# A Mamba-2 mixer with a LoRA-routed linear layer on one core: two chunks of 256 tokens instead of four of 128, and another order of the products in a step

## The chip, the cores and the metric

The kernel runs on one core of a Trainium2 chip. Its time is the device time of one execution in microseconds. Engines are named as in the profile: PE is TensorE (matmul), PEld its weight loads, DVE is VectorE, ACT is ScalarE, POOL is GpSimd, SP is SyncE, which here only issues DMAs.

## What is computed

The input x is 2 x 512 tokens of 512 values. With xn its layer norm, the output is `x + mamba2(xn) + lora_linear(xn)`.

```python
proj = hidden_states @ in_proj_w.T                  # 512 -> 8192 gate + 10240 hBC + 128 dt
hBC = silu(causal_conv4(hBC) + conv_b)              # hs 8192, B 8 x 128, C 8 x 128
dt = softplus(dt + dt_bias)
A_cs = cumsum(A * dt, within a chunk)
Y_diag = (C B^T * exp(segsum(A dt))) @ (hs * dt)    # inside a chunk
states = (B * exp(A_cs[last] - A_cs))^T @ (hs * dt) # one 128 x 64 state per head and chunk
Y_off = (C @ state_before_the_chunk) * exp(A_cs)
y = Y_diag + Y_off + D * hs
xg = y * silu(gate)
out = (xg * rsqrt(mean over a group of 1024 (xg^2) + eps) * norm_weight) @ out_proj_w.T
```

There are 128 heads of 64 channels and 8 groups of B and C. The second summand is `xn @ W.T + b` plus a LoRA product whose rank (8, 16, 32 or 64) a softmax over four scores picks for each token. The length of a chunk is a free choice: the recurrence gives the same result for any.

## The kernel before

A batch (there are 2, index b) is one sequence of 512 tokens. All its tokens lie side by side in the free dimension, so most operations are 512 columns wide. A large product is made in three parts from high and low halves in fp32r (`three`, L505: hi x hi, hi x lo, lo x hi, each in KT = 4 blocks, twelve PE instructions). `project` (L519) makes 128 channels of the input projection for 512 tokens. Scans, states, score and Y products and transposes are in fp32. Every matmul in fp32 is two PE instructions in the profile, a transpose is one.

A **prologue** per batch makes dt, its soft log and the cumulative sums (`csT`, by a scan over `chunked`, which restarts every 128 tokens), the LoRA part, and for 8 groups g the conv of B and C and the **scores** (L558, score products `bo[2]<-h2,ct`, masked on DVE by `causal` into `gt`). Tables by token follow: `cs_tok`, `dt_tok`, `dd_tok` (decay to the chunk's end times dt) and `cd_bc` (decay over a chunk).

The **step loop** has 64 steps per batch, two heads (128 channels) each. It is software pipelined: PE's pass m, called slot m here, holds the projections of step m, the scan of step m-1 and the output product of step m-2. Each engine runs its own list of instructions in the order in which they are written, with semaphores between them; that order is all that sets what stands behind what. In a slot PE does (before the change):

1. **hs** product, `project(bh, ...)`, L509 by its helper's line, then **states**: `bt<-xd,btok` (L635), one 128x128 product for each of the first three chunks (NS = 3), then **Y**, `by<-mt,xt` (L641): for four blocks j of 128 tokens and two heads h a product with 64 stationary columns, into the upper or lower half of the bank;
2. **gate** product, `project(bg, ...)`, then **off**: `bt<-ct,S` (L657), three products of 128 columns with the running states S;
3. after every eighth step the sums of squares, `bt<-ones,sqa` (L662), into the last columns of `bt`;
4. **output** product of step m-2, `bo<-woh,xh` and the two mixed ones (L676), twelve instructions, accumulated over eight steps in four banks bo;
5. four **transposes** of the conv's result, `bt<-ident,h` (L687; the tile `h2` is printed as `h`).

[...]

DVE does in slot m: `xd` and `xt` (L868, L873), conv taps (L701), running states `next_state` (L726), y1 = D * hs + Y (L894), `silu_conv` (L707), the gate's `sg` (L908), `yo`, its addition and `xg` (L915, L918, L922), the **mask** mt * gt (L928, both heads in one instruction), and after each group `add_group` (L719), which empties the four output banks into `acc`. ACT does the last tap (L282), eight Relu pieces of the decay exponents (`rises`, L291), exp over them (L390), tanh of conv and gate (L287, L401), the copy of the first state S (L385), the high halves `xh`, `woh`, `wh` (L364, L407, L278), the norm weight on the output weights (L396) and the squares (L370). POOL makes the low halves `xl`, `wol`, `wl` (L479, L491, L440), the sum of squares (L486) and the inverse root (L446). SP issues the loads of weights and of the rows `cs_row` and `ec_row`, broadcast from DRAM.

## Time and profile before

| | us |
|---|---|
| median of 3 runs (lowest, highest) | 1695.9 (1695.87, 1696.78) |
| the profiled execution | 1696.02 |
| its span in the trace | 1694.3 |
| PE busy | 1644.4 (97%) |
| DVE, ACT, POOL busy | 1352.8, 1191.2, 1089.1 |

Matmuls overlap: a row of n of them lasts from the start of the first to the end of the last, and the time from one row's start to the next row's start is what they cost PE. A timeline merges neighbouring instructions of the same line, operation and tile into one row with their count. "idle before" in brackets is the time for which the engine had nothing to do ahead of the row, and what ended it.

### The profile page before, as it was taken

Reading aid. Unit: us, or ns where it says so; the run is one execution under the profiler, and the core shown is the slowest. Engines: PE = TensorE matmul, PEld = TensorE weight load, DVE = VectorE, ACT = ScalarE, POOL = GpSimd, SP = SyncE. Lnnn points to the kernel's source line nnn. Section 1 sums busy time; section 2 is a strip of 40 time slices with the busy share of each in tenths; the row PEclk is TensorE's granted clock in tenths of the full one; section 3 lists DMA queues with packets and bytes.
Section 4 is the critical chain, followed back from the end, with each engine's and each line's share of the span. In section 5 each row is a group of like instructions: output and inputs, shape, how many; then the busy total and the mean of one; then the engine's idle time right before and its main releaser. Section 6 shows DMA issues by size and latency. Waiting matters only on the chain.

```text
span 1694.3 us, 28881 instructions
## 1 busy us (share of the span) xinstructions
PE 1644.4 (97%) x9694; PEld 1355.9 (80%) x9694; DVE 1352.8 (80%) x2388; ACT 1191.2 (70%) x2442; POOL 1089.1 (64%) x1384
## 2 busy tenths in 40 slices
PE   6999999999999999999899999999999999999996
PEld 5778888888888888887787788888888888888885
DVE  5987788878787888878889878888788878787875
ACT  2577777777777777777635777777777777777773
POOL 5346676676676677676663466776766676676673
PEclk9999999999999999999999999999999999999998
DMA  4243444343444344343123433443443443443331
GB/s 150 65 143 123 140 136 129 130 144 122 129 144 127 125 144 131 120 144 131 58 86 100 156 128 124 144 131 120 144 132 122 142 133 120 142 133 126 136 119 36
DMA packets 82146, 212.03 MB, mean 125 GB/s; under 512 B 11024, under 2 KB 27408, under 8 KB 81744
## 3 DMA queue, kind: packets, MB, share of 16 engines
q1 hardware_dynamic: 82000, 210.20, 38.1%
q8 instruction: 78, 1.28, 0.3%
q14 instruction: 68, 0.56, 0.1%
HBM read 207.01 MB, written 3.15 MB: 124 GB/s over the span
## 4 chain that ended last, share of the span: by engine, by line
PE 69%; DVE 19%; ACT 6%; issue 5%; POOL 0%; DMA 0%; SPq 0%; DVEq 0%; ACTq 0%; POOLq 0%
PE bg L509 18%; PE bh L509 16%; PE bo L676 15%; DVE cv L701 6%; PE by L641 6%; PE bt L635 4%; PE bt L657 4%; DVE mt L928 2%; PE bt L687 2%; DVE acc L719 2%; ACT raw_o L396 1%; ACT mt L390 1%; DVE xt L873 1%; ACT cv L282 1%; DVE by L918 1%
## 5 line engine op out<-in xcount | busy, mean ns | idle before, releaser
L440 POOL TENSOR_TENSOR wl<-raw,wh 128x256 fp32r<-128x256 f32 x584 | 530.6, 939 | 101.5 <-ACT wh L278 101.5
L491 POOL TENSOR_TENSOR wol<-raw_o,woh 128x256 fp32r<-128x256 f32 x256 | 184.3, 741 | 468.6 <-ACT woh L407 468.6
L701 DVE SCALAR_TENSOR_TENSOR cv<-bh,par_sb,cv 128x511 f32<-128x511 f32 (+2 forms) x408 | 304.6, 747 | 140.2 <-ACT cv L282 135.1
L291 ACT ACTIVATE mt<-cs_row,cs_tok 128x128 f32<-128x128 f32 x1024 | 324.4, 389 | 0.0
L676 PE MATMUL bo<-woh,xh 128*128 128x512 f32 x512 | 213.7, 417 | 0.0
L676 PE MATMUL bo<-woh,xl 128*128 128x512 f32 x512 | 202.6, 396 | 0.0
L676 PE MATMUL bo<-wol,xh 128*128 128x512 f32 x512 | 200.9, 392 | 0.0
L908 DVE SCALAR_TENSOR_TENSOR sg<-tg,bg 128x512 f32<-128x512 f32 x128 | 88.1, 688 | 140.6 <-ACT tg L401 140.6
L287 ACT ACTIVATE bh<-cv 128x512 f32<-128x512 f32 x136 | 81.9, 602 | 159.2 <-DVE cv L701 159.2
L479 POOL TENSOR_TENSOR xl<-xg,xh 128x256 fp32r<-128x256 f32 x256 | 181.7, 730 | 4.9 <-ACT xh L364 4.9
L364 ACT ACTIVATE xh<-xg 128x512 fp32r<-128x512 f32 x128 | 81.0, 633 | 142.8 <-DVE xg L922 142.8
L928 DVE TENSOR_TENSOR mt<-mt,gt 128x1024 f32<-128x1024 f32 x128 | 174.1, 1360 | 0.0
L509 PE MATMUL bh<-xTh,wh 128*128 128x512 f32 x552 | 163.8, 419 | 1.5 <-DVE xTl L759 1.5
L509 PE MATMUL bg<-xTh,wh 128*128 128x512 f32 x544 | 161.8, 419 | 0.0
L486 POOL TENSOR_TENSOR sqa<-sqa,sq 128x256 f32<-128x256 f32 x224 | 160.6, 738 | 0.0
L278 ACT ACTIVATE wh<-raw 128x1024 fp32r<-128x1024 f32 (+1 forms) x146 | 152.8, 1046 | 0.7 <-DMA raw<-in_w_dtag 0.7
L282 ACT ACTIVATE cv<-bh,par_sb 128x512 f32<-128x512 f32 x136 | 105.7, 777 | 66.3 <-PE bh L509 61.3
L509 PE MATMUL bh<-xTl,wh 128*128 128x512 f32 x552 | 150.6, 395 | 0.0
L509 PE MATMUL bh<-xTh,wl 128*128 128x512 f32 x552 | 148.7, 391 | 0.0
L509 PE MATMUL bg<-xTl,wh 128*128 128x512 f32 x544 | 146.8, 391 | 0.0
L509 PE MATMUL bg<-xTh,wl 128*128 128x512 f32 x544 | 146.2, 390 | 0.0
L641 PE MATMUL by<-mt,xt 128*64 128x128 f32 x2048 | 141.0, 280 | 0.0
(159 smaller groups left out, 3328.3 us busy)
## 6 DMA issues: line engine op xcount, KB each, us to landing
raw<-in_w_step SPq DMA_DIRECT2D x128, 512.0 KB, 3.7
cs_row<-cs_rows SPq DMA_DIRECT2D x128, 512.0 KB, 4.5
raw_o<-in_w_out SPq DMA_DIRECT2D x128, 256.0 KB, 2.7
ec_row<-ec_rows SPq DMA_DIRECT2D x256, 96.0 KB, 3.7
raw<-in_w_bc SPq DMA_DIRECT2D x16, 512.0 KB, 3.6
acc<-in_x SPq DMA_DIRECT2D x2, 1024.0 KB, 5.7
mt<-in_w_ffn SPq DMA_DIRECT2D x2, 1024.0 KB, 6.7
out_dram<-acc SPq DMA_DIRECT2D x2, 1024.0 KB, 4.6
```

Source lines behind the costliest of these rows:

```text
L278: act.activation(wh[:, n % 2, 0:width(n)], raw[:, n % 2, 0:width(n)], ACT.Copy).then_inc(a_wh, 1)
L282: act.activation(cv[:, u, :], src[:, :], ACT.Identity, bias=par_sb[:, un % UNITS, TAPS:TAPS + 1], scale=par_sb[:, un % UNITS, TAPS - 1:TAP ...
L291: e = act.activation(mt[:, m % 2, h, chunk(j)], cs_row[:, m % 2, h, chunk(j)], ACT.Relu, bias=cs_tok[:, b, j, 2 * m + h:2 * m + h + 1], sc ...
L440: e = pool.tensor_tensor(wl[:, n % 2, part], raw[:, n % 2, part], wh[:, n % 2, part].bitcast(F32), ALU.subtract)
L479: e = pool.tensor_tensor(xl[:, u, part], xg[:, u, part], xh[:, u, part].bitcast(F32), ALU.subtract)
L486: e = pool.tensor_tensor(sqa[:, part], sqa[:, part], sq[:, part], ALU.add)
L491: e = pool.tensor_tensor(wol[:, 1 - u, part], raw_o[:, 1 - u, part], woh[:, 1 - u, part].bitcast(F32), ALU.subtract)
L509: mm = pe.matmul(dst, a(k), c(k), start=(n == 0 and k == 0), stop=(stop and n == 2 and k == KT - 1))
L641: mm = pe.matmul(by[HD * h:HD * (h + 1), chunk(j)], xt[:, j, HD * h:HD * (h + 1)], mt[:, 1 - u, h, chunk(j)], start=True, stop=True)
L676: mm = pe.matmul(bo[j][:, :], a[:, u, chunk(j)], c[:, u, :], start=(first and k == 0), stop=False, skip_group_check=True)
L701: dve.scalar_tensor_tensor(out=cv[:, u, k:], in0=src[:, 0:L - k], scalar=par_sb[:, un % UNITS, TAPS - 1 - k:TAPS - k], in1=cv[:, u, k:], o ...
L928: dve.tensor_tensor(mt[:, u], mt[:, u], gt[:, m % GROUPS, :].unsqueeze(1).broadcast_to([P, 2, L]), ALU.mult).then_inc(v_m, 1)
```

## The change

A chunk is now CL = 256 tokens long, so there are NC = 2 chunks. One state remains, that of the first chunk, so `next_state` and `cd_bc` go. `span(j)` is the block of query tokens that key block j reaches: 256 columns for the first block of a chunk, 128 for the second. `tri(j)` is its place in the packed lower triangle of TRI = 384 columns per chunk, in which `mt`, `gt` and `causal` now lie. Y accumulates two key blocks in the same columns. Off and what follows it (`yo`, its addition) cover the second chunk's 256 tokens alone, and off now goes to `bg`.

The hs product alternates between banks bh and bt (`mine`, `other`); states and transposes follow it there. On PE a slot's three fp32r products stand in a row, and all fp32 products behind them. DVE does yo, its addition and xg of step m-2 at the start of slot m and not at the end of slot m-1; the mask of step m-1 comes a slot later; the gate's sg ahead of the conv's h2; y1 last. ACT has the last tap ahead of the squares, both tanh after the first Relu pieces, and the copy of S behind tanh, norm scale and woh. POOL splits the next step's weights (`split_lo`) one step later and ahead of wol. In the prologue score products use the wider `span(j)`, transposes of B are two, the tables by token are made in three groups rather than two, and are no longer kept per batch. The four token transposes of the next batch and its `ag` product take the place of a projection in the last two slots; its norm statistics come a slot later.

```diff
@@ sizes and places
-NS = NJ - 1
+CL = 2 * P
+NC = L // CL
+TRI = CL + P
+        def span(j):
+            return slice(P * j, CL * (j // 2) + CL)
+        def tri(j):
+            return slice(TRI * (j // 2) + CL * (j % 2), TRI * (j // 2) + (CL if j % 2 == 0 else TRI))
@@ scores, PE
-                    mm = pe.matmul(bo[2][:, chunk(j)], h2[:, u, chunk(j)], ct[:, g, chunk(j)], start=True, stop=True)
+                    mm = pe.matmul(bo[2 + j // 2][:, CL * (j % 2):CL * (j % 2) + (P if j % 2 else CL)],
+                                   h2[:, u, chunk(j)], ct[:, g, span(j)], start=True, stop=True)
...
@@ step loop, PE
                     if has(m):
                         pe.wait_ge(p_wl, did(step(b, m)))
-                        project(bh, b, step(b, m) % 2, 0).then_inc(t_hs, 1)
+                        project(mine, b, step(b, m) % 2, 0).then_inc(t_hs, 1)
+                        if has(m - 2):
+                            pe.wait_ge(v_off, did(n - 2))
                         project(bg, b, step(b, m) % 2, 1).then_inc(t_g, 1)
+                    elif b + 1 < NB:
+                        pe.wait_ge(v_off, did(n - 2))
+                        if m == STEPS:
+                            for j in range(NJ):
+                                turn_tokens(b + 1, j)
+                        else:
+                            project_ag(b + 1)
...
                     if has(m - 2):
...
                         mm.then_inc(t_out, 1)
+                    if ends and m < STEPS:
+                        pe.wait_ge(v_sg, did(n))
+                        sum_squares(bg)
+                    if has(m - 1):
...
+                        for c in range(2):
+                            mm = pe.matmul(other[:, 0:P], btok[:, g, c, :], xd[:, c, :], start=(c == 0), stop=(c == 1))
+                        mm.then_inc(t_st, 1)
+                        pe.wait_ge(v_m, did(n - 1))
+                        pe.wait_ge(v_xg, did(n - 2))
+                        for j in range(NJ):
+                            for h in range(2):
+                                mm = pe.matmul(by[HD * h:HD * (h + 1), span(j)], xt[:, j, HD * h:HD * (h + 1)],
+                                               mt[:, 1 - u, h, tri(j)], start=(j % 2 == 0), stop=(j % 2 == 1),
+                                               skip_group_check=True)
+                        mm.then_inc(t_d, 1)
                     if m == STEPS and b + 1 < NB:
                         project_dt(b + 1)
+                    if has(m - 1):
+                        pe.wait_ge(v_sg, did(min(n, b * STEPS + STEPS - 1)))
+                        pe.wait_ge(v_off, did(n - 2))
...
+                        pe.wait_ge(a_s1, did(n - 1))
+                        pe.matmul(bg[:, CL:], S[:, :], ct[:, g, CL:], start=True, stop=True).then_inc(t_off, 1)
                     if has(m):
                         pe.wait_ge(v_h2, did(un))
                         for j in range(NJ):
-                            mm = pe.transpose(bt[:, chunk(j)], h2[:, u, chunk(j)], ident[:, :])
+                            mm = pe.transpose(mine[:, chunk(j)], h2[:, u, chunk(j)], ident[:, :])
                         mm.then_inc(t_t, 1)
@@ POOL
+                    if m >= -1 and (has(m + 1) or (m < STEPS + 1 and b + 1 < NB)):
+                        split_lo(step(b, m + 1))
                     if has(m - 1):
                         pool.wait_ge(a_woh, did(n - 1))
...
-                    if m + 2 < STEPS or (m < STEPS and b + 1 < NB):
-                        split_lo(step(b, m + 2))
```

On PE an ordinary slot of the step loop read so before (`woh`, `wol`, `xh`, `xl` are the output product's halves; eleven more rows like the last belong to it, and the four transposes come behind them):

```order
L509 MATMUL bh<-xTh,wh 128x512 [waits v_h2,p_wl]
L635 MATMUL bt<-xd,btok 128x128 [waits v_x,v_xd]
L635 MATMUL bt<-xd,btok 128x128 x2
L641 MATMUL by<-mt,xt 64x128 [waits v_xg,v_m]
L641 MATMUL by<-mt,xt 64x128 x7
L509 MATMUL bg<-xTh,wh 128x512 [waits v_sg]
L657 MATMUL bt<-ct,S 128x128 [waits v_s]
L657 MATMUL bt<-ct,S 128x128 x2
L676 MATMUL bo<-woh,xh 128x512 [waits p_wol,p_xl]
```

and reads so now:

```order
L516 MATMUL bh<-xTh,wh 128x512 [waits p_wl]
L516 MATMUL bg<-xTh,wh 128x512 [waits v_off,v_sg]
L670 MATMUL bo<-woh,xh 128x512 [waits p_wol,p_xl]
L683 MATMUL bt<-xd,btok 128x128 [waits v_x,v_xd]
L683 MATMUL bt<-xd,btok 128x128
L689 MATMUL by<-mt,xt 64x256 [waits v_xg,v_m]
L689 MATMUL by<-mt,xt 64x256
L689 MATMUL by<-mt,xt 64x128 x2
L689 MATMUL by<-mt,xt 64x256 x2
L689 MATMUL by<-mt,xt 64x128 x2
L701 MATMUL bg<-ct,S 128x256 [waits a_s1,v_off,v_sg]
L705 MATMUL bh<-ident,h 128x128 [waits v_h2]
```

Gate and output moved ahead of states, Y and off; states and off lost two matmuls each, half of Y's are wider, and off now waits for ACT's copy of S (a_s1) itself.

On ACT the same slot before, from the squares on:

```order
L370 ACTIVATE sq<-xg 128x512 [waits p_sqa]
L291 ACTIVATE mt<-cs_row,cs_tok 128x128 [waits t_d,ld_cs1]
L291 ACTIVATE mt<-cs_row,cs_tok 128x128 x3
L282 ACTIVATE cv<-bh,par_sb 128x512 [waits v_h2,t_hs]
L385 ACTIVATE S<-bt 128x128 [waits t_off,t_st]
L291 ACTIVATE mt<-cs_row,cs_tok 128x128 x4
L287 ACTIVATE bh<-cv 128x512 [waits v_tap]
L390 ACTIVATE mt<-mt 128x1024 [waits a_rl]
L396 ACTIVATE raw_o<-raw_o,par_sb 128x512 [waits ld_rawo0]
L401 ACTIVATE tg<-bg 128x512 [waits v_sg,t_g]
L407 ACTIVATE woh<-raw_o 128x512 [waits t_out,a_wn]
```

and now, where the rows of the second four Relu pieces (L299, like the first) and of exp over 1536 columns (L414) follow the last:

```order
L290 ACTIVATE cv<-bt,par_sb 128x512 [waits v_h2,t_hs]
L390 ACTIVATE sq<-xg 128x512 [waits p_sqa]
L299 ACTIVATE mt<-cs_row,cs_tok 128x256 [waits t_d,ld_cs1]
L299 ACTIVATE mt<-cs_row,cs_tok 128x128
L299 ACTIVATE mt<-cs_row,cs_tok 128x256
L299 ACTIVATE mt<-cs_row,cs_tok 128x128
L397 ACTIVATE tg<-bg 128x512 [waits v_sg,t_g]
L295 ACTIVATE bt<-cv 128x512 [waits v_tap]
L403 ACTIVATE raw_o<-raw_o,par_sb 128x512 [waits ld_rawo0]
L407 ACTIVATE woh<-raw_o 128x512 [waits t_out,a_wn]
L410 ACTIVATE S<-bh 128x128 [waits t_off,t_st]
```

The copy of S stood between the last tap and the second Relu pieces; it now stands behind the tanh that waits for DVE's taps, and behind norm scale and woh.

## Rows read from the trace of the kernel before

**Rows 1.** The page: busy time and share; granted clock in 40 slices; chain by engine.
```profile
PE 1644.4 (97%) x9694; PEld 1355.9 (80%) x9694; DVE 1352.8 (80%) x2388; ACT 1191.2 (70%) x2442; POOL 1089.1 (64%) x1384
PEclk9999999999999999999999999999999999999998
PE 69%; DVE 19%; ACT 6%; issue 5%; POOL 0%; DMA 0%; SPq 0%; DVEq 0%; ACTq 0%; POOLq 0%
```

**Rows 2.** Timeline, one ordinary slot, PE: start us, length us, engine, line, operation.
```profile
432.47 1.18 PE L509 MATMUL bh<-xTh,wh 128*128 128x512 f32 x4
...
435.34 0.91 PE L635 MATMUL bt<-xd,btok 128*128 128x128 f32 x6
...
436.17 1.09 PE L641 MATMUL by<-mt,xt 128*64 128x128 f32 x16
...
437.20 1.19 PE L509 MATMUL bg<-xTh,wh 128*128 128x512 f32 x4
...
440.05 0.83 PE L657 MATMUL bt<-ct,S 128*128 128x128 f32 x6
...
440.64 0.48 PE L676 MATMUL bo<-woh,xh 128*128 128x512 f32 x1
...
443.49 0.60 PE L687 MATMUL bt<-ident,h 128*128 128x128 f32 x4
...
443.85 0.48 PE L509 MATMUL bh<-xTh,wh 128*128 128x512 f32 x1
```

**Rows 3.** Timeline, three slots around the end of a group, PE and DVE.
```profile
385.89 1.18 PE L509 MATMUL bh<-xTh,wh 128*128 128x512 f32 x4
...
394.16 0.95 PE L662 MATMUL bt<-ones,sqa 128*128 128x1 f32 x8
...
398.17 1.17 PE L509 MATMUL bh<-xTh,wh 128*128 128x512 f32 x4
...
399.73 2.72 DVE L719 SCALAR_TENSOR_TENSOR acc<-bo,rr,acc 128x512 f32<-128x512 f32 x4
...
409.46 1.17 PE L509 MATMUL bh<-xTh,wh 128*128 128x512 f32 x4
```

**Rows 4.** Timeline, prologue of batch 0, PE: wide fp32, a projection behind another, scores.
```profile
54.45 3.70 PE L596 MATMUL bo<-w_b_sb,gt 64*128 64x512 f32 x8
...
60.97 1.07 PE L509 MATMUL bg<-xTh,wh 128*128 128x512 f32 x4
...
63.69 1.05 PE L558 MATMUL bo<-ct,h 128*128 128x128 f32 x8
```

**Rows 5.** Groups by line and shape, DVE: count, busy us, mean ns, idle before.
```profile
L928 DVE TENSOR_TENSOR mt<-mt,gt 128x1024 f32<-128x1024 f32 x128 | 174.1, 1360 | 0.0
L726 DVE SCALAR_TENSOR_TENSOR S<-S,cd_bc,bt 128x64 f32<-128x64 f32 x512 | 118.8, 274 | 4.3 <-ACT S L385 4.2
L701 DVE SCALAR_TENSOR_TENSOR cv<-bh,par_sb,cv 128x511 f32<-128x511 f32 x136 | 101.8, 749 | 135.1 <-ACT cv L282 135.1
...
L915 DVE TENSOR_TENSOR yo<-bt,ec_row 128x384 f32<-128x384 f32 x128 | 70.5, 551 | 0.4 <-PE bt L657 0.4
```

**Rows 6.** The same view, ACT.
```profile
L291 ACT ACTIVATE mt<-cs_row,cs_tok 128x128 f32<-128x128 f32 x1024 | 324.4, 389 | 0.0
...
L396 ACT ACTIVATE raw_o<-raw_o,par_sb 128x512 f32<-128x512 f32 x128 | 90.4, 706 | 0.0
L287 ACT ACTIVATE bh<-cv 128x512 f32<-128x512 f32 x136 | 81.9, 602 | 159.2 <-DVE cv L701 159.2
...
L407 ACT ACTIVATE woh<-raw_o 128x512 fp32r<-128x512 f32 x128 | 79.3, 619 | 0.1
...
L385 ACT ACTIVATE S<-bt 128x128 f32<-128x128 f32 x128 | 35.0, 273 | 15.4 <-PE bt L635 15.4
...
L356 ACT ACTIVATE cd_bc<-bo 128x256 f32<-128x256 f32 x2 | 0.8, 387 | 0.0
```

**Rows 7.** Timeline, PE, a slot near the end of batch 0.
```profile
806.24 1.62 PE L635 MATMUL bt<-xd,btok 128*128 128x128 f32 x6 [2.87 <-DVE xt L873]
```

**Rows 8.** Timeline, PE, the last sums of squares.
```profile
1679.79 1.65 PE L662 MATMUL bt<-ones,sqa 128*128 128x1 f32 x8 [2.75 <-POOL sqa L486]
```

More of the change, by code:

```diff
@@ L290, in rises @@
                 for j in range(NJ):
-                    e = act.activation(mt[:, m % 2, h, chunk(j)], cs_row[:, m % 2, h, chunk(j)], ACT.Relu,
-                                       bias=cs_tok[:, b, j, 2 * m + h:2 * m + h + 1], scale=-1.0)
+                    e = act.activation(mt[:, m % 2, h, tri(j)], cs_row[:, m % 2, h, span(j)], ACT.Relu,
+                                       bias=cs_tok[:, j, 2 * m + h:2 * m + h + 1], scale=-1.0)
                 e.then_inc(a_rl, 1)
@@ L330, in _ @@
                 act.activation(ecT, csT, ACT.Exp).then_inc(pa, 1)
[L331 to L334 removed]
+                act.activation(dec, csT[:, 0:CL], ACT.Exp, scale=-1.0, bias=csT[:, CL - 1:CL]).then_inc(pa, 1)
                 act.wait_ge(pe_, b * PRO_PE + PE_UT)
@@ L473, in _ @@
                     n, u = b * STEPS + m, m % 2
-                    if m == STEPS - 3 and b + 1 < NB:
+                    if m == STEPS - 2 and b + 1 < NB:
                         inverse_dev(b + 1)
@@ L616, in _, with sum_squares @@
                     n, un, u = b * STEPS + m, b * UNITS + 2 * GROUPS + m, m % 2
+                    mine, other = bank_s[u], bank_s[1 - u]
+                    ends = has(m - 2) and (m - 2) % PER_GROUP == PER_GROUP - 1
+                    def sum_squares(dst):
+                        pe.wait_ge(p_sqa, squares(b, m - 2))
+                        for j in range(NJ):
+                            mm = pe.matmul(dst[:, j:j + 1], sqa[:, chunk(j)], ones[:, 0:1],
+                                           start=True, stop=True)
+                        mm.then_inc(t_ss, 1)
@@ L793, in decays_and_route @@
                 dve.wait_ge(p_xl, did(b * STEPS - 1))
-                link(b, dve.tensor_tensor_scan(csT, chunked[:, :], dh, 0.0, ALU.mult, ALU.add))
+                for c in range(NC):
+                    part = slice(CL * c, CL * (c + 1))
+                    link(b, dve.tensor_tensor_scan(csT[:, part], ones[:, 0:1].broadcast_to([P, CL]), dh[:, part], 0.0,
+                                               ALU.mult, ALU.add))
                 assert done[b] == PRO_DVE_CS
```

335 lines of the change are left out of this document (143 added, 192 removed).

## The prediction

> **What bounds the kernel now.** I read the page's first and fourth parts first: TensorE has work 97% of the span at full clock, and its instructions carry 69% of the chain that ended last [rows 1]. Busy PE is not by itself proof, so I then followed one slot of the step loop on PE [rows 2]. Its seven phases follow one another without a gap: hs product 2.87 us, states 0.83, Y 1.03, gate product 2.85, off-diagonal 0.59, output product 2.85, transposes 0.36, together 11.38. Over the 128 slots the ordinary ones take 11.32 to 11.40 by the same two starts, mean 11.35; in every other one the states begin some 0.05 late, behind xt. DVE and ACT are busy 80% and 70% and wait inside the slot. So a PE instruction saved is time saved, for as long as nobody comes late to PE. Twice per group of eight steps a slot is longer: by 0.9 where the squares are summed, which costs PE 0.82, and then by about 0.35 where DVE empties the four output banks (slots of 12.28 and 11.29, then 11.72, counted from hs product to hs product) [rows 3].
>
> **What the change does to a slot on PE.** All fp32r products (hs, gate, output) now stand in one row, the fp32 ones (states, Y, off, transposes) in one row behind them.
>
> (1) States: three 128-column fp32 products become two. A product is two PE instructions here (768 records for 384 products). Eight such instructions in a row last 1.05 in all and one lasts 0.27, so they start 0.111 apart [rows 4]; six in 0.59 is 0.098 apiece [rows 2]. Two fewer: −0.21.
> (2) Off: three products of 128 columns become one of 256. Width 512 in fp32 is in the trace: eight instructions over 3.70, one lasting 0.59, so 0.44 apart, four times the narrow one's [rows 4]. A 256-column one then takes 0.21 to 0.22 and the pair 0.43, against 0.59: −0.16.
> (3) Y: sixteen 64x128 instructions in 1.03 [rows 2], 0.064 each, under the 0.107 that one of this width needs, so the two heads' halves of the array run side by side, eight pairs of 0.107. Four of the eight pairs get 256 columns: +4 × 0.107 = +0.43. The bounds: +0.34 if some of the 1.03 is fixed start-up hidden by wider ones, +0.64 if the two halves overlap only in part once their widths alternate. I take 0.43, since pairs are what the row shows.
> (4) Changes of kind. A projection that follows another starts its next three blocks 2.72 later (60.97 to 63.69) [rows 4], behind an fp32 phase the same blocks take 2.85; the output product takes 2.85 there too, of which its first instruction is 0.31 long instead of 0.23. Gate and output now follow fp32r work: −0.13 and −0.08. The hs product still follows the transposes and keeps its extra 0.1.
> (5) The 0.05 wait for xt goes: xt is now made some 6 us before the states want it. −0.04.
>
> Sum per slot: −0.21 −0.16 +0.43 −0.13 −0.08 −0.04 = −0.19; built up from the new order instead (2.84 + 2.72 + 2.77 + 0.56 + 1.46 + 0.43 + 0.36) it is 11.14, −0.21. I take −0.21: **128 × −0.21 = −27 us**. From the bounds of (3) and of (4) (nothing to −0.3): −0.33 to +0.05.
>
> Y still needs the array cut into two halves and put together again. Between the end of the pairs and the next phase there is about 0.1 that no product fills (16 instructions need 0.86 of the 1.03) [rows 2], and I leave it in. [...]
>
> **Who could come late.** Let 0 be the start of a slot's hs product; PE then starts gate at 2.8, output 5.6, states 8.3, Y 8.9, off 10.3, transposes 10.8, next slot 11.1.
> DVE. Off the list: 4 state updates of 0.23 net (four in 0.93) and a third of three 384-wide operations (0.55 to 0.42). Mask: 1.36 for 1024 columns becomes 1.9 to 2.0 for 1536 [rows 5]. Its new order is y1 behind Y (ready 10.4), yo, add, xg (to 1.4 of the next slot), xd, xt (2.35), mask (4.3), three taps of 0.75 (6.55), sg, h2 (7.9). It then idles 2.5.
> ACT. Eight Relu pieces of 0.39, half of them now 256 wide: 128 to 256 columns costs 0.11 at most by its row of 0.387 against 0.273 for a PSUM copy of 128, and up to double if I scale; exp of 1536 columns costs +0.43. So 9.4 becomes some 10.3 busy in 11.1 [rows 6]. Its queue is strict: gate tanh, **tanh of the conv (waits for the taps)**, norm scale, woh, **the copy of S**, and only then can PE do off. In an ordinary slot: taps ready 6.55, tanh to 7.15, scale and woh to 8.4, S waits for the states until 9.0, ready 9.3, against 10.3 wanted. A slack of 1.0, so nothing is paid.
> POOL: xl ready about 4, wanted 5.6; the split of the next step's weights (four of 0.94) moves ahead of wol and ends near 9.6, wanted 11.1. SP's weight load goes behind that split, near 9.6, and its 3.7 us to landing end 10 us before ACT wants it. Both hide.
>
> **(6) The slot in which the banks are emptied.** DVE does 4 × 0.68 = 2.7 more between xt and the mask [rows 3]. Taps end 9.25, tanh 9.9, scale 10.5 (0.71), woh 11.1 (0.62), S ready 11.4: off waits 1.05 to 1.1. Before, the same work cost 0.35 a slot later. 14 such slots (7 a batch): **14 × 0.72 = +10 us**. If the wait eats less, say 0.5, it is +2; the slot after it recovers (ACT is done with exp at 2.0, before the mask at 2.35).
> (7) Prologue of a batch: the score products cover 768 instead of 512 columns, +4 × 0.107 for each of 8 groups; one transpose less in each, −0.11; the products that spread the chunk decays go, −0.54 with one transpose. 2 × (8 × 0.32 − 0.54) = **+4 us**. PE is about as loaded there as DVE, whose mask grows by about as much.
> (8) End of batch 0. The slots where DVE also makes the next batch's norms are 14.3, 13.9 and 12.7, 6.9 over the ordinary; the first shows PE waiting 2.87 for xt [rows 7]. DVE has 1 us more room in each: I get some 3.3. Then all four token transposes stand ahead of the output product, two round trips PE-ACT-DVE-PE, with DVE's mask behind: +1.4. Net **−2 us**.
> (9) The very end. The last step's output product but one stood behind off and was hidden under the chain yo, xg, xh, xl, squares, for which PE waited 2.75 at the end [rows 8]. Now it stands ahead of the last states and off, in the chain: **+2.7 us**, its length.
>
> Sum: −27 +10 +4 −2 +2.7 = −12.3. The profiled execution took 1696.0 (span 1694.3), the median of the three runs 1695.9, so no correction is needed: **1684 us**.
>
> **Rivals.**
> A, *ACT's queue sets every slot* (slower). What (6) prices for 14 slots happens in all: from Y's end through y1, yo, add, xg, xd, xt, mask, taps, tanh, scale, woh, S to off is one chain of about 10.1 us round the loop, with 1.0 of slack. For it: ACT becomes 93% busy, and ten operations stand in that chain, each of which may be dearer than I take it. Against: no single wait in the walk is over. It decides once the chain is 1 us longer than I count; each 0.1 above costs 13 us. With 0.3 above: −12 + 38, 1722.
> B, *Y widens by 0.64 instead of 0.43* (slower): +0.21 × 128 = +27, 1711. For it: alternating widths and instructions that start in order. Against: both heads of a token block have the same width.
> C, *the changes of kind were not what cost the extra 0.2* (no change or slightly slower): gate and output keep their long first instruction, for instance since it is a first instruction after a semaphore wait. −12 + 27 = +15, 1711; if half stays, 1697, no change. Against: blocks that follow without such a change take 2.72 with a semaphore wait ahead of them as well.
> D, *more is won*: (6) is half hidden and Y costs 0.34: −12 −5 −11, 1668.
>
> **How the numbers follow.** Forecast with the size of (3), (4) and (6) as taken, 1677 to 1691: 0.50. D and between: 0.12. C's half, about 1697: 0.12. B, or C in full, 1700 to 1712: 0.14. A: 0.12. The predicted time is the first one's. Leaving out A and the far side of D gives 1667 to 1710. A measurement of this kernel tells some 0.2% (3.4 us) from no change: faster 0.62, same 0.12, slower 0.26.
>
> **What would show it.** Right: ordinary slots of 11.1 to 11.2 with phases 2.72 for gate, 2.75 for output, 0.43 for off, 1.45 for Y; the slots with emptied banks about 12.1, off waiting for ACT's S. Wrong: PE waiting for S in ordinary slots (A); Y at 1.65 (B); the first instruction of gate and output still 0.3 (C).

## The result, and the profile of the changed kernel

The change makes the kernel 0.2% slower. It takes 1699.95 us (median of 20 runs, 1697.19 to 1702.32), the kernel before beside it 1696.22 (20 runs, 1694.20 to 1699.27); the ratio is 1.0018, with a 95% interval of 1.0012 to 1.0025. The forecast was 1684, faster. The time lies in the range of the prediction, but the sign is wrong. The profiled execution of the changed kernel has a span of 1699.5. Of the experiments below, one execution of e2 (2336.4) and one of e3 (3308.5) were far slower than all others; they stand in no median.

The page, as [rows 1]: PE has lost 794 instructions and 10.5 us of busy time, and the span is longer all the same. The last slice of the granted clock has fallen from 8 to 7.
```profile
PE 1633.9 (96%) x8900; PEld 1316.1 (77%) x8900; DVE 1284.7 (76%) x1894; ACT 1327.9 (78%) x2436; POOL 1141.9 (67%) x1383
PEclk9999999999999999999989999999999999999997
PE 79%; DVE 12%; issue 4%; ACT 2%; POOL 2%; DMA 0%; SPq 0%; DVEq 0%; ACTq 0%; POOLq 0%
```

The timeline of one ordinary slot on PE, as [rows 2] (start, length, engine, line, operation):
```profile
444.89 1.17 PE L516 MATMUL bh<-xTh,wh 128*128 128x512 f32 x4
...
447.74 1.07 PE L516 MATMUL bg<-xTh,wh 128*128 128x512 f32 x4
...
450.46 0.39 PE L670 MATMUL bo<-woh,xh 128*128 128x512 f32 x1
...
453.21 0.60 PE L683 MATMUL bt<-xd,btok 128*128 128x128 f32 x4
453.74 1.52 PE L689 MATMUL by<-mt,xt 128*64 128x256 f32 x16
455.19 0.70 PE L701 MATMUL bg<-ct,S 128*128 128x256 f32 x2
455.73 0.60 PE L705 MATMUL bh<-ident,h 128*128 128x128 f32 x4
456.08 1.17 PE L516 MATMUL bt<-xTh,wh 128*128 128x512 f32 x4
```
From start to start: hs 2.85, gate 2.72, output 2.75, states 0.53, Y 1.45, off 0.54, transposes 0.35. That is 11.19 against a mean of 11.35 before: 0.16 gained in a slot, where 0.21 was forecast.

What PE waits for (microseconds in all, times, longest):
```profile
PE bg L701 <- ACT S L410: 17.1, 16, 1.1
...
PE bo L670 <- POOL xl L486: 7.7, 4, 5.0
PE bo L516 <- DVE acc L734: 2.5, 1, 2.5
```
Off waits for the copy of S in 16 slots: the 14 of the prediction's step (6), and in each batch the second slot, which it had not seen. The last row is the wait at the turn (e7). No ordinary slot waits for it.

**Where the time went.** I cut both kernels at the start of a step's transposes, T(0) to T(63) in each batch. Of both there is a second profile (e10 is before, e9 after), and the columns give both executions. T is the start of the instructions of L687 before and of L705 after.

| stretch | before, e10 | after, e9 | difference | predicted |
|---|---|---|---|---|
| start to T(0) of batch 0 | 110.78, 113.56 | 115.75, 113.56 | +2.2, see below | +2.0 |
| T(0) to T(1), each batch | 10.82, 10.85 | 9.61, 9.61 | 2 x -1.2 | 2 x -0.2 |
| T(1) to T(60), batch 0 | 678.41, 678.49 | 673.98, 674.11 | -4.4 | -7.4 |
| T(60) to T(63) | 40.96, 39.73 | 37.03, 37.06 | -3.3 | -3.9 |
| T(63) to T(0) of batch 1 | 103.69, 103.71 | 112.31, 112.36 | +8.6 | +3.2 |
| T(1) to T(63), batch 1 | 712.50, 712.44 | 707.78, 707.83 | -4.7 | -8.0 |
| T(63) to the end | 26.25, 26.18 | 33.44, 32.52 | +6.8 | +2.7 |

The differences sum to +2.8, the medians to +3.7; the last column sums to -11.8, the prediction's -12.3. The start must be compared at a like clock (the clock of TensorE that the profile shows as granted, as a share of full speed). The records of it hold two values, 1.00 and 0.50, and no other in the twelve traces that have them. Between 28 and 36 us both kernels can run at 0.50 for a while (after from 29.0 to 35.8 us, before not at all, but e10 from 29.7 to 36.5), by chance between executions (columns: busy time and instructions of PE, PEld, DVE, ACT, POOL, then the granted clock). First before, then e10, after and e9:
```profile
28.00:36.00 8.00, 8.00 (x49) 7.08 (x49) 7.83 (x6) 1.35 (x2) 4.58 (x6) 1.00 0.01 2
```
```profile
28.00:36.00 8.00, 8.00 (x40) 7.42 (x40) 7.30 (x7) 1.70 (x3) 2.27 (x4) 0.60 0.01 2
```
```profile
28.00:36.00 8.00, 8.00 (x37) 7.39 (x37) 7.70 (x7) 1.34 (x2) 2.25 (x4) 0.57 0.01 2
```
```profile
28.00:36.00 8.00, 8.00 (x41) 6.91 (x41) 7.83 (x6) 1.34 (x2) 4.97 (x6) 0.79 0.01 2
```
T(0) follows it: 110.78 at 1.00 and 113.56 at 0.60 before; 113.56 at 0.79 and 115.75 at 0.57 after. At 0.60 and 0.57 the change costs 2.2. Half of the 5 us that the first two profiles show there is chance.

So the miss of some 15 has three large parts: the slots (+6.3), the turn from batch 0 to batch 1 (+5.4) and the end (+4.1), less 2.0 gained in the second slots. The experiments take them one by one.

### The profile page after: what moved, and what is told of

It reads as the page before. It is cut to its first block, busy times and chain, and to the rows that moved or that the text cites. A ratio compares the mean times of both kernels' runs of the same rounds, so it can differ in the third digit from the quotient of the medians.

```text
span 1699.5 us, 26818 instructions
## 1 busy us (share of the span) xinstructions
PE 1633.9 (96%) x8900; PEld 1316.1 (77%) x8900; DVE 1284.7 (76%) x1894; ACT 1327.9 (78%) x2436; POOL 1141.9 (67%) x1383
## 4 chain that ended last, share of the span: by engine, by line
PE 79%; DVE 12%; issue 4%; ACT 2%; POOL 2%; DMA 0%; SPq 0%; DVEq 0%; ACTq 0%; POOLq 0%
PE bg L516 19%; PE bo L670 18%; PE bt L516 10%; PE by L689 9%; PE bh L516 9%; PE bg L701 4%; DVE cv L717 4%; DVE acc L734 2%; DVE mt L906 2%; PE bh L683 2%; PE bh L705 2%; PE bo L516 1%; PE bt L683 1%; PE bt L705 1%; PE bo L565 1%
## 5 line engine op out<-in xcount | busy, mean ns | idle before, releaser
L486 POOL TENSOR_TENSOR xl<-xg,xh 128x256 fp32r<-128x256 f32 x256 | 332.0, 1316 | 364.9 <-ACT xh L375 364.9
L299 ACT ACTIVATE mt<-cs_row,cs_tok 128x256 f32<-128x256 f32 (+1 forms) x1024 | 379.2, 443 | 0.0
L906 DVE TENSOR_TENSOR mt<-mt,gt 128x1536 f32<-128x1536 f32 x128 | 229.0, 1789 | 2.1 <-ACT mt L414 2.1
L689 PE MATMUL by<-mt,xt 128*64 128x256 f32 (+1 forms) x2048 | 194.7, 332 | 0.0
L414 ACT ACTIVATE mt<-mt 128x1536 f32<-128x1536 f32 x128 | 190.6, 1489 | 4.1
L717 DVE SCALAR_TENSOR_TENSOR cv<-bh,par_sb,cv 128x511 f32<-128x511 f32 (+2 forms) x216 | 161.3, 747 | 12.7 <-ACT cv L290 7.4
L689 PEld LDWEIGHTS by<-mt,xt 128*64 128x64 f32 x2048 | 126.8, 136 | 52.4
L717 DVE SCALAR_TENSOR_TENSOR cv<-bt,par_sb,cv 128x511 f32<-128x511 f32 (+2 forms) x216 | 161.5, 748 | 5.4
L516 PEld LDWEIGHTS bg<-xTh,wh 128*128 128x128 f32 x544 | 101.9, 188 | 21.9 <-issue 0.8
L516 PEld LDWEIGHTS bg<-xTh,wl 128*128 128x128 f32 x544 | 102.1, 188 | 21.3
```

The lines of the kernel that those rows point to most:

```text
L299: e = act.activation(mt[:, m % 2, h, tri(j)], cs_row[:, m % 2, h, span(j)], ACT.Relu, bias=cs_tok[:, j, 2 * m + h:2 * m + h + 1], scale=-1.0)
L414: act.activation(mt[:, u], mt[:, u], ACT.Exp, scale=-1.0).then_inc(a_ex, 1)
L486: e = pool.tensor_tensor(xl[:, u, part], xg[:, u, part], xh[:, u, part].bitcast(F32), ALU.subtract)
L516: mm = pe.matmul(dst, a(k), c(k), start=(n == 0 and k == 0), stop=(stop and n == 2 and k == KT - 1))
L689: mm = pe.matmul(by[HD * h:HD * (h + 1), span(j)], xt[:, j, HD * h:HD * (h + 1)], mt[:, 1 - u, h, tri(j)], start=(j % 2 == 0), stop=(j % 2 ...
L717: dve.scalar_tensor_tensor(out=cv[:, u, k:], in0=src[:, 0:L - k], scalar=par_sb[:, un % UNITS, TAPS - 1 - k:TAPS - k], in1=cv[:, u, k:], o ...
```

## Experiments

Times stand against the kernel before on the same chip (1696.4 to 1696.6 in all three series). Where a kernel ran in several rounds it has a ratio with its interval. "Under the kernel after" compares with its 1699.95, which was measured beside a kernel before of 1696.22. The kernel after itself varies by 5 us between executions, so such a difference is good to 1 or 2 us, and the traces decide where it lies.

### e1: S copied ahead of the conv's tanh where it is late

In the slots whose output banks are emptied, and in a batch's second slot, ACT copies S between its two tanh instead of behind woh.
```diff
                         act.activation(tg[:, :], bg[:, :], ACT.Tanh, scale=0.5).then_inc(a_tg, 1)
+                        if early:
+                            copy_state(n, other)
                         tanh_conv(un, u, mine)
...
-                        act.activation(S[:, :], other[:, 0:P], ACT.Copy).then_inc(a_s1, 1)
+                        if not early:
+                            copy_state(n, other)
```


> The changed kernel, with ACT's copy of S placed between the two tanh instead of behind woh, in the 14 slots in which DVE empties the output banks and in slot 1 of each batch. Theory 1 (ACT's queue holds the copy behind the conv's taps): off waits 1.07 us for S in those 16 slots of the changed kernel, S is then ready at 9.3 against 10.3 wanted, the wait goes whole: -17 us, 1683, clearly below the kernel before. Rival (the wait moves): conv tanh and h2 come later by the copy and the slot is then held by h2 or by the mask, half or less is won: 1692 to 1700.

Measured: 1689.62, ratio 0.9957 (0.9945 to 0.9969), 10.3 under the kernel after. The mechanism of step (6) is shown: ACT's queue made PE wait. This is ACT in such a slot of the kernel after, where S is ready on PE at 407.9 and its copy stands behind three operations, the first of which waits for the taps,
```profile
404.82 0.60 ACT L397 ACTIVATE tg<-bg 128x512 f32<-128x512 f32 x1
408.26 0.60 ACT L295 ACTIVATE bh<-cv 128x512 f32<-128x512 f32 x1 [2.84 <-DVE cv L717]
408.80 0.71 ACT L403 ACTIVATE raw_o<-raw_o,par_sb 128x512 f32<-128x512 f32 x1
409.54 0.63 ACT L407 ACTIVATE woh<-raw_o 128x512 fp32r<-128x512 f32 x1
410.07 0.26 ACT L410 ACTIVATE S<-bt 128x128 f32<-128x128 f32 x1
```
and PE at the other end of it:
```profile
410.48 0.67 PE L701 MATMUL bg<-ct,S 128*128 128x256 f32 x2 [1.07 <-ACT S L410]
```
But not all of the 17 us came back. In e1 the slot with emptied banks still is 11.7 long, and PE waits for another engine:
```profile
PE bo L677 <- POOL xl L493: 11.8, 20, 5.0
```
Behind the wait for S stood the next one, for POOL's xl. It makes 16 slots some 0.5 us longer than an ordinary one (by the profile's count 0.26 of it is idle time).

### e3: the mask on DVE behind the taps

The same chain from its other end: DVE makes the mask only after the taps and sg, so ACT's tanh need not wait for it.
```diff
-                    if has(m - 1):
+                    def mask():
...
+                    if has(m - 1) and not has(m):
+                        mask()
...
                                                  op0=ALU.add, op1=ALU.mult).then_inc(v_sg, 1)
+                        if has(m - 1):
+                            mask()
```


> The changed kernel, with DVE's mask of a step placed behind the taps and the gate's sg instead of ahead of the taps. Theory 3 (POOL's xl takes 1.32 us a piece instead of 0.73 because DVE's mask runs beside it): xl falls to 0.75 a piece, whatever POOL works beside the mask then (wl) becomes dearer. Ordinary slots stay at 11.19. In the slots with emptied banks off no longer waits for S, but Y waits 0.7 to 0.9 for the mask, and the slots with sums of squares wait 0.6 for sg: 1698 to 1706. Rival for xl (it is dear because ACT reads and writes the same tiles beside it): xl stays at 1.3.

Measured: 1706.98, ratio 1.0054 (1.0039 to 1.0068), 1 us over the top of what was expected. The trace is of another execution of the same kernel:

> The same kernel as e3 (the mask on DVE behind the taps and sg), for a trace of it. Theory (xl on POOL takes 1.3 us a piece instead of 0.73 because DVE's mask, two operands from SBUF, runs beside it): with the mask elsewhere xl is near 0.75, what stands beside the mask then gets the slow pieces (wol or wl), and the loss of 7 us against the kernel after comes from ordinary or emptied slots in which PE waits for the mask or for xg behind it. Rival (xl is slow for another reason, for instance its place behind wol): xl stays at 1.3.

It took 1702.97. Ordinary slots are 11.26 (+0.07, where none was expected), emptied ones 11.95 (-0.33), in them PE now waits for the mask, and in batch 0's second slot 2.6 for it. The second slots are where most is lost: 12.79 and 11.20 instead of 9.61.
```profile
PE by L689 <- DVE mt L906: 16.4, 18, 2.6
```
The wait for S has become one for the mask, nearly as large in all (16.4 against 17.1). What the run settles is why xl is slow. Groups on POOL (count, busy us, mean ns, idle before): first of before,
```profile
L440 POOL TENSOR_TENSOR wl<-raw,wh 128x256 fp32r<-128x256 f32 x582 | 530.1, 941 | 101.5 <-ACT wh L278 101.5
...
L479 POOL TENSOR_TENSOR xl<-xg,xh 128x256 fp32r<-128x256 f32 x256 | 181.7, 730 | 4.9 <-ACT xh L364 4.9
```
of after,
```profile
L447 POOL TENSOR_TENSOR wl<-raw,wh 128x256 fp32r<-128x256 f32 x582 | 435.0, 778 | 113.9 <-ACT wh L286 113.9
L486 POOL TENSOR_TENSOR xl<-xg,xh 128x256 fp32r<-128x256 f32 x256 | 332.0, 1316 | 364.9 <-ACT xh L375 364.9
```
and of e3b:
```profile
L447 POOL TENSOR_TENSOR wl<-raw,wh 128x256 fp32r<-128x256 f32 x582 | 575.2, 1020 | 111.1 <-ACT wh L286 111.1
...
L486 POOL TENSOR_TENSOR xl<-xg,xh 128x256 fp32r<-128x256 f32 x256 | 184.6, 742 | 304.2 <-ACT xh L375 304.2
```
Whatever POOL does beside the mask is slow. The mask stood beside wl before, stands beside xl after, and beside wl again in e3b: the mean piece of xl takes 730, 1316 and 742 ns, the mean piece of wl 941, 778 and 1020. These means mix two kinds of piece. In the ordinary slot shown above the mask runs from 447.24 to 448.99. The piece of xl that starts at 447.37 takes 2.21 us, the next one, which starts when the mask is over, 0.74:
```profile
L486 POOL TENSOR_TENSOR xl<-xg,xh x2: 737/1475/2213, 447.4 to 449.5; 128x256 fp32r<-128x256 f32 x2
```
(shortest, median, longest in ns; first and last start). So POOL all but stands still while the mask runs: of the 2.21 us, 0.59 lie behind its end, which leaves some 0.15 of a piece's 0.74 for the 1.62 beside it (my estimate from these times). Of the 256 pieces of xl, 140 miss the mask and take 0.74, the 116 that meet it take 2.02 in the mean.

### e2: the last output product behind the last off

In batch 1 there is no next slot to hide it, and step (9) priced it at its length.
```diff
-                    if has(m - 2):
+                    def output():
...
+                    late = m == STEPS and b + 1 == NB
+                    if has(m - 2) and not late:
+                        output()
...
                         pe.matmul(bg[:, CL:], S[:, :], ct[:, g, CL:], start=True, stop=True).then_inc(t_off, 1)
+                    if late:
+                        output()
```


> The changed kernel, with the output product of step 62 placed behind off in the last slot of batch 1, where it stood before the change. Theory 2 (the end was lengthened because this product, and POOL's xl for which it waits, now stand ahead of the last states): states begin some 8 us earlier, the product is hidden under the chain yo, xg, xh, xl, squares: -6 us, 1694. Rival (the end is set by the clock and the last chain alone): -0 to -2, 1698 to 1700.

Measured: 1693.23, ratio 0.9975 (0.9964 to 0.9985), 6.7 under the kernel after; its tail is 25.7 instead of 33. In the kernel after the product waits 4.97 for xl, and then runs at a granted clock of 0.50:
```profile
1671.65 0.80 PE L670 MATMUL bo<-woh,xh 128*128 128x512 f32 x1 [4.97 <-POOL xl L486]
1672.24 0.63 PE L670 MATMUL bo<-wol,xh 128*128 128x512 f32 x1
...
1685.20 1.87 PE L631 MATMUL bt<-ones,sqa 128*128 128x1 f32 x8 [5.25 <-POOL sqa L493]
```
The twelve blocks take 5.28, 0.43 apiece, where they take 2.73 at a clock of 1.00. In e9 the same wait is followed by six such blocks only, and the twelve take 4.24 at a mean clock of 0.65. POOL's two pieces of xl took 2.92 beside the mask (2.24):
```profile
1668.67 2.92 POOL L486 TENSOR_TENSOR xl<-xg,xh 128x256 fp32r<-128x256 f32 x2 [3.15 <-ACT xh L375]
```
In e2 states start at 1667.39 instead, off at 1672.21, and the same product begins behind it at 1672.87.

The moved product is only a part of these 6.7 us. Counted from T(63), the last sums of squares begin after 11.8 in the kernel before (both executions), 19.1 and 17.8 after, 14.2 in e2; from there to the end it is 14.3 to 14.8 in before, e10, after and e9, and 11.5 in e2. So the change lost 6.0 and 7.3, all of it ahead of the sums; the edit takes 3.6 to 4.9 of that back. The rest of what e2's profile gains, 2.9 to 3.3, is clock: over the last sums and the output product behind them it is 0.52, 0.52, 0.55 and 0.50 in before, e10, after and e9, and 1.00 in e2. And 2.4 stay lost in e2: Y waits 1.38 for the mask and then takes 2.76 at a clock of 0.50, not 1.45.

### e4: states between gate and output

In the kernel after fp32r work ends with the output product and is taken up again behind the transposes. This puts two fp32 products in its midst.
```diff
...
+                        for c in range(2):
+                            mm = pe.matmul(other[:, 0:P], btok[:, g, c, :], xd[:, c, :], start=(c == 0), stop=(c == 1))
+                        mm.then_inc(t_st, 1)
                     if has(m - 2):
                         first = (m - 2) % PER_GROUP == 0
...
-                        for c in range(2):
-                            mm = pe.matmul(other[:, 0:P], btok[:, g, c, :], xd[:, c, :], start=(c == 0), stop=(c == 1))
-                        mm.then_inc(t_st, 1)
```


> The changed kernel, with the states of a slot placed between the gate and the output product, so that a slot has two rows of fp32 products instead of one, and one more change from fp32 back to fp32r. Theory 4 (such a change costs PE about 0.1, as the first instruction behind it shows): ordinary slots 11.29, +12 us, 1712. Rival (C of the prediction, it costs nothing by itself): 11.19, 1700.

Measured: 1694.98, ratio 0.9980 (0.9968 to 0.9991). One reading expected a loss of 12, the rival no change, and it gains 5. An ordinary slot is 11.19 as in the kernel after; the added pair of changes costs nothing in sum:
```profile
449.82 0.60 PE L666 MATMUL bt<-xd,btok 128*128 128x128 f32 x4
450.18 0.48 PE L679 MATMUL bo<-woh,xh 128*128 128x512 f32 x1
...
452.77 0.39 PE L679 MATMUL bo<-woh,xl 128*128 128x512 f32 x1
453.09 1.52 PE L690 MATMUL by<-mt,xt 128*64 128x256 f32 x16
454.54 0.70 PE L702 MATMUL bg<-ct,S 128*128 128x256 f32 x2
```
Output takes 2.91, 0.17 more than in the kernel after, and its first instruction is long again. In return states take 0.36 instead of 0.53, though it is the same four instructions. The starts of single instructions show why (medians over the ordinary slots). The first output instruction is 0.31 ahead of the second, where the others are 0.23 apart; but it also starts 0.03 behind the last one of the states, where another fp32 instruction would start 0.11 behind it. In sum the change from fp32 to fp32r costs 0.01, and the early start is why states take only 0.36. What output pays stands at its end: the last output instruction starts 0.32 ahead of Y (452.77 to 453.09), not 0.23. In the kernel after, the last instruction of the states starts 0.20 ahead of Y, and 0.11 ahead of it in e6 below, where Y takes the whole array. So going into the two halves costs 0.09, the same behind fp32 as behind fp32r.

The gain of 5 is 14 x 0.21 in the slots with emptied banks (12.06 instead of 12.28), where off waits 0.82 instead of 1.07 (the mask there takes 1.75 instead of 1.97); 14 x 0.12 in the slots with sums of squares (11.97 instead of 12.09); and 0.8 between T(60) and T(63).

### e5 and e6: Y narrow, and Y over the whole array

e5 leaves out the part of Y that goes from the first half of a chunk to the second. e6 adds the second head onto the first with all 128 stationary columns, which is another sum than the reference's.
```diff
-                                mm = pe.matmul(by[HD * h:HD * (h + 1), span(j)], xt[:, j, HD * h:HD * (h + 1)],
-                                               mt[:, 1 - u, h, tri(j)], start=(j % 2 == 0), stop=(j % 2 == 1),
-                                               skip_group_check=True)
+                                own = slice(tri(j).start, tri(j).start + P)
+                                mm = pe.matmul(by[HD * h:HD * (h + 1), chunk(j)], xt[:, j, HD * h:HD * (h + 1)],
+                                               mt[:, 1 - u, h, own], start=True, stop=True)
```
```diff
-                                mm = pe.matmul(by[HD * h:HD * (h + 1), span(j)], xt[:, j, HD * h:HD * (h + 1)],
-                                               mt[:, 1 - u, h, tri(j)], start=(j % 2 == 0), stop=(j % 2 == 1),
-                                               skip_group_check=True)
+                                mm = pe.matmul(by[:, span(j)], xt[:, j, :],
+                                               mt[:, 1 - u, h, tri(j)], start=(j % 2 == 0 and h == 0),
+                                               stop=(j % 2 == 1 and h == 1), skip_group_check=True)
```


> The kernel after, but Y's products for a block of 128 tokens read only the block's own 128 columns of the mask table instead of 256 for every other block; the part of Y that goes from the first half of a chunk to the second is left out, everything else stays. Theory (the two halves of the array run side by side, a wider pair costs four times 0.107): Y's phase goes from 1.45 to 1.02-1.05 us and the ordinary slot from 11.19 to 10.76, unless another engine comes late; 114 ordinary slots at -0.43 are -49, so near 1651. Rival (B, the pairs overlap only in part, +0.64): Y goes to 0.81, slot 10.55. A second rival, ACT's queue (exp 1.5, eight rises, 93% busy) or the loop through Y, the mask and S sets the slot once PE needs 0.43 less: slot stays above 10.9 and PE waits for S or for the mask in ordinary slots.

> The kernel after, but Y's 16 instructions use all 128 stationary columns (both heads of a block of tokens at once, the second head added onto the first, so Y is another sum than the reference's) instead of a half of the array each. It asks what cutting the array costs. Theory (states 0.54, off 0.53 hold 0.17 and 0.10 that belong to going into the two halves and out of them): Y takes 4 x 2 x (0.107 + 0.214) = 2.56 us, states fall from 0.54 to 0.36 and off from 0.53 to 0.43, slot 11.19 + 1.11 - 0.28 = 12.0, time near 1700 + 114 x 0.83 = 1795. Rival (the 0.17 and 0.10 are what any phase costs that follows fp32r products or Y): states 0.54 and off 0.53 stay, slot 12.3, near 1826.

Measured, one execution each: e5 1650.16, e6 1816.75. In e5 Y takes 1.02 (454.95 to 455.97) and the slot 10.76:
```profile
454.95 1.09 PE L690 MATMUL by<-mt,xt 128*64 128x128 f32 x16
455.97 0.70 PE L701 MATMUL bg<-ct,S 128*128 128x256 f32 x2
```
The width costs 0.43, as step (3) had it; B is excluded. And the other engines, ACT's queue among them, follow a slot of 10.76: rival A was not near. Only the slots with emptied banks give less, 12.07 against 12.28; there the wait for S grows to 1.5. In e6:
```profile
456.03 0.60 PE L683 MATMUL bt<-xd,btok 128*128 128x128 f32 x4
456.47 2.78 PE L689 MATMUL by<-mt,xt 128*128 128x256 f32 x16
459.09 0.60 PE L701 MATMUL bg<-ct,S 128*128 128x256 f32 x2
459.52 0.60 PE L705 MATMUL bh<-ident,h 128*128 128x128 f32 x4
```
States take 0.44 and off 0.43, each at the price of its columns (4 and 2 x 2 times 0.107). Going into the two halves costs 0.1 (0.54 less 0.44) and leaving them 0.1 (0.54 less 0.43) in the phases beside Y. Inside Y there is more: its last instruction starts 0.20 ahead of off, where the pairs follow each other by 0.11. The slot is 12.18, between the two expectations: Y took 2.62, not 2.56, and states kept 0.08 more than I had allowed them (0.36 is what they take ahead of an fp32r product, which starts early); but both phases beside Y fell, which the rival excludes.

### e7: off ahead of the next batch's dt product

```diff
-                    if m == STEPS and b + 1 < NB:
-                        project_dt(b + 1)
                     if has(m - 1):
+                        if m == STEPS and b + 1 < NB:
+                            pe.wait_ge(pv, (b + 1) * PRO_DVE + PRO_DVE_XT)
...
                         pe.matmul(bg[:, CL:], S[:, :], ct[:, g, CL:], start=True, stop=True).then_inc(t_off, 1)
+                    if m == STEPS and b + 1 < NB:
+                        project_dt(b + 1)
```


> The kernel after with one edit at the end of batch 0: off of the last step stands ahead of the next batch's dt product instead of behind it. In the kernel after ACT takes up dt only at 852.9, 3.3 us after PE has finished it, since the last step's xh and sq stand ahead in ACT's queue and wait for xg, and xg waits for off behind the dt product; DVE's long chain on dt ends at 870.9 and PE waits 2.46 for it, then runs at a clock of 0.66. Theory: xg comes 2.8 earlier, DVE's chain starts near 852.0 instead of 854.84, the wait of 2.46 is gone and with it the low clock: -2.8 to -4.2, near 1696. Rival (the chain is set by ACT's exp and the norm work, or the prologue is bound by PE later on and takes the gain back): within 1 us of the kernel after.

Measured: 1696.00, ratio 0.9997 (0.9987 to 1.0007), 4 under the kernel after; from T(63) to T(0) 108.10 instead of 112.3. In the kernel after PE is done with dt at 849.56, but ACT takes it up at 852.90 (L326), since xh and sq, both made from xg, stand ahead of it:
```profile
851.84 0.63 ACT L375 ACTIVATE xh<-xg 128x512 fp32r<-128x512 f32 x1 [6.21 <-DVE xg L883]
...
852.90 0.67 ACT L326 ACTIVATE cs_row<-bh,hp 128x512 f32<-128x512 f32 x1
```
xg needs off, and off stood behind the dt product. DVE's chain on dt then begins at 854.84, where it began at 854.83 in the kernel before: all that the slots had gained by then is gone. At its end PE waits, and the next two rows of four blocks behind the first run at half speed (1.7 between starts, not 0.91; the granted clock is 0.50 from 872.1 to 875.5):
```profile
871.06 1.19 PE L516 MATMUL bo<-xTh 128*128 128x512 f32 x4 [2.46 <-DVE acc L734]
872.07 1.89 PE L516 MATMUL bo<-xTl,xTh 128*128 128x512 f32 x4
```
In e7 ACT has it at 850.61, and PE goes on 2.3 earlier and at a clock of 1.00:
```profile
849.54 0.63 ACT L375 ACTIVATE xh<-xg 128x512 fp32r<-128x512 f32 x1 [3.49 <-DVE xg L885]
...
850.61 0.69 ACT L326 ACTIVATE cs_row<-bh,hp 128x512 f32<-128x512 f32 x1
```
```profile
868.77 1.16 PE L516 MATMUL bo<-xTh 128*128 128x512 f32 x4 [0.52 <-DVE acc L736]
```
Counted from T(63), that product starts 2.7 earlier. The remaining 1.5 of the 4.2 is the low clock: e2 and e3b leave the turn as it is, have the same wait of 2.5 and a clock of 1.00 behind it, and take 110.80 and 110.75.

### e9 and e10: both kernels once more

> The kernel after once more, for the granted clock between 28 and 36 us and in the last 30 us. In its first profile it is 0.57 in 28-36 us, and 0.68 in 1670-1700. If the dip at the start belongs to the kernel, it is again 0.55 to 0.65 and the first transposes of the step loop stand at about 115.7 us; if it is chance between executions, it can be 1.00 and they stand near 113.4.

> The kernel before once more, for the granted clock between 28 and 36 us (1.00 in its first profile) and in the last 30 us (0.79). If the dip of the kernel after belongs to its own start, it is 1.00 again; if it is chance between executions, it may be below.

1698.39 and 1697.59. The clock in 28 to 36 us was 0.79 and 0.60, so the dip at the start is no property of the change.

### e8: all four edits that won

The edits of e1, e2, e4 and e7 in one kernel.

> All edits that won alone, together on the kernel after: the copy of S between the two tanh in the slots whose banks are emptied and in a batch's second slot (-10.3 alone), the last output product behind the last off (-6.7), states between gate and output (-5), off ahead of dt (-3.5). The states edit saved mostly S waits, which the first takes as well; but it puts 0.36 ahead of the output product, which with the first edit waits some 0.5 for xl in 14 slots. Theory: 1700 - 10.3 - 6.7 - 3.5 - 1 - 14 x 0.35 = 1674 to 1678. Rival (the edits share one and the same slack, so that no more than the best two add up): 1681 to 1684.

Measured: **1669.97**, ratio 0.9842 (0.9827 to 0.9856): 1.6% under the kernel before, 30 us under the kernel after. Neither expectation was low enough. The largest waits on PE that are left:
```profile
PE bh L540 <- DVE gt L776: 11.5, 1, 11.5
PE bh L540 <- DVE xTl L781: 5.1, 2, 4.0
PE bo L572 <- DVE gt L850: 4.7, 4, 1.3
PE bt L673 <- DVE xt L913: 2.7, 2, 2.3
```
S is gone from the whole list, and of xl one wait of 1.4 is left, in the last slot. The slot with emptied banks is 11.19 like any other: e1 alone left 0.55 in it, for xl, e4 puts 0.36 of other work ahead of the output product, and together nothing is left. Against the kernel after, T(1) to T(60) is 8.3 shorter, T(1) to T(63) of batch 1 8.5, the second slots 2.2, the turn 4.3, the end 5.5 to 6.4. The 16 waits for S alone are 17.

## Why the prediction failed, step by step

**(1), (2), (3): right.** Two products less at the states, off at 0.43 for its columns, Y +0.43: e5 and e6 show each of these prices.

**(4), the changes of kind: the sum was too high by 0.05 a slot, 6 us, and the cause it gave for gate was wrong.** Gate and output did lose their 0.13 and 0.10. But off, costed at 0.43, takes 0.54. The prediction kept the 0.1 at the end of Y's pairs in Y's phase; that the phase behind Y pays another 0.1, whichever it is, was not in its sum. The starts of single instructions bear it out. The first instruction behind Y is 0.34 ahead of the next when it is gate's (before; 0.23 in an fp32r row), and 0.32 when it is off's (after; 0.22 in e6, where nothing is tiled). So gate's long first instruction was the price of leaving the two halves, 0.11 at gate and 0.10 at off, and the change only hands it on to off, where it disappears in e6: off takes 0.43 there. What a change from fp32 to fp32r costs is small: 0.01 at the change (e4), and some 0.04 where the blocks behind it are 0.231 apart in the median instead of 0.227 (in e4's output product they are 0.227). Gate, behind Y, and output had such blocks before, and that much they did save. Output's long first instruction was the other side of an off that ended 0.08 early, so its -0.08 and the -0.16 of step (2) are together the price of off's narrower work.

**(5): right.** No ordinary slot waits for xt.

**(6): right in place and size.** Off waits 1.07 for S in the predicted 14 slots. The three slots of a group from the sums of squares on are 1.98 over three ordinary ones, before 1.26, so 14 x 0.72 = +10, as forecast. What it missed is the second slot of each batch, which has the same wait. There it is paid for: before, the transposes of that slot waited 1.7 to 1.8 for yo, which shared a bank with them, and with alternating banks they don't. The sum of it is a gain of 1.2 a batch instead of 0.2.
```profile
PE bt L687 <- DVE yo L915: 3.5, 2, 1.8
```

**(7): right.** +2.2 in the prologue of batch 0, once the clock is the same.

**(8): wrong by 5.4.** The slots at the end of batch 0 gave 3.3 in all, 0.6 less than forecast. The turn behind them was priced at +1.4 for two round trips of the token transposes. The waits there are 1.04, 0.98 and 0.52, so that much was near. Not seen was that off now stands behind the dt product, and that ACT's queue ties the dt chain to off through xg, xh and sq. That is 4.2 (e7): 2.7 because the chain starts later, and 1.5 because PE, after its wait, runs at the low clock. Of the seven profiles with that wait four have a mean clock of 0.66 over the next 5 us (after, e9, e1, e4), and e2, e3b and e6 have 1.00. The prediction followed its own rule about ACT's strict queue in the slots, and did not apply it here.

**(9): wrong by 4.** The output product in the chain was priced at its length, 2.7. The end became 6.8 longer: the product also waits for xl of the step before, which nothing hides in the last slot; xl is slow beside the mask; and after 4.97 us of idle PE (4.98 in e9) all or half of it runs at 0.43 a block instead of 0.23. Putting the product back (e2) takes 3.6 to 4.9 of it off; 2.4 are not its doing but the mask's, for which Y now waits in the last slot, and Y's low clock. That e2's medians differ by 6.7, as much as the whole loss, is chance.

**POOL.** "xl ready about 4, wanted 5.6" was wrong: it is ready at 5.4, since it took the place beside the mask that wl had. It just holds in ordinary slots (wanted 5.6), and is what limits e1. The row for it was in the trace of before (wl 941 ns, the other operations of the same shape near 735), and I read it as wl's own price.

**The rivals.** A is excluded by e5, B by e5 and e6. C, that the first instructions after fp32 stay long, didn't happen as told, but its half, "1697, no change", is nearest to what came in time, but by luck: what stays of the 0.2 is 0.1 at off, and the rest of the miss lies elsewhere. No rival had the turn and the end in it, which together are the larger part of the miss.

Open is why the clock at 28 to 36 us and at the turn differs between executions of one kernel, and why the blocks of a product behind fp32 work are 0.231 apart, but 0.227 in e4's output product.

## What to carry to other kernels

When products are moved in a loop, walk its first and its last pass as carefully as the middle: in every queue, ask what now stands behind the moved instruction and who waits for that. Here 0.16 us times 128, 20 us, was won in the ordinary order of a slot; 10 went, as forecast, in 14 slots, and 13 at two places that occur once, of which 4 were forecast. A wait of 1 us on a strict queue is cheap to remove once its place is known: one copy moved up was worth 10 us, and it paid in full only when the next in line (xl) was covered too. Before you move a large DVE operation like this mask (1536 columns, both operands in SBUF), look which operations of another engine run beside it. Here they were the slow ones: xl, 1316 ns in the mean after and 742 in e3b, or wl, 1020 in e3b and 778 after.

## What the runs showed of the hardware

- Going into half-array tiles costs PE 0.09 us, behind fp32 (0.205 in the kernel after instead of 0.112 in e6 from the last instruction to Y) and behind fp32r (0.318 instead of 0.227, e4). Leaving them costs 0.10 at the last tiled instruction (0.20 in the kernel after instead of 0.11 in e6) and 0.10 in the next phase, whether fp32 (0.32 in the kernel after instead of 0.22 in e6) or fp32r (0.335 instead of 0.227, before).
- From fp32 to fp32r in the whole array the first block is 0.09 longer (0.314 instead of 0.227, e4) and starts 0.08 earlier (0.031 instead of 0.11), 0.01 in sum; the blocks behind it are 0.231 apart in the median instead of 0.227 (hs, gate and output before, hs after), and 0.227 in e4's output product.
- A POOL operation on 256 columns that meets DVE's 1536-column product of two SBUF operands takes 2.02 in the mean and 2.31 at most in the kernel after, instead of 0.74; where POOL is at work when the product starts (19 of 128), the product is slower too, 1.97 in the median (1.95 to 2.26) against 1.75.
- After a wait of 4.97 us PE ran twelve blocks in 5.28 instead of 2.73 (mean clock 0.50, after), after one of 4.98 in 4.24 (0.65, e9). After one of 2.46 in the kernel after it ran at a clock of 0.66 for 5 us (from 871 on), after one of 2.48 in e9 too (from 869 on), and at 1.00 in e2, e3b and e6 behind the same 2.5 us wait.
